# A decoder of two layers on one core: third late projection tile inside attention, POOL's bias adds moved, expert output banks counted free earlier

## The chip, the cores and the metric

One core of one Trainium2 chip runs the kernel. Times are device microseconds (us) of one execution. The kernel is compared by the median of several executions.

## The reference

x has 2 batches of 1024 rows and 256 columns; a context has 2 batches of 77 rows. Six sublayers follow one another, each `x = layernorm(x + sublayer(x))`:

```python
x = _layernorm(x + _L0_attn_ref(...))    # quaternion projections, 16 heads, softmax over 1024 keys
x = _layernorm(x + _L0_xattn_ref(...))   # two hops of memory attention over the context
x = _layernorm(x + _L0_ffn_ref(...))     # 8 experts: gelu(tok @ w1 + b1) @ w2 + b2, 256 rows each
x = _layernorm(x + _L1_attn_ref(...))    # long convolution, gelu, projection, layer norm
x = _layernorm(x + _L1_xattn_ref(...))   # 16 heads, keys and values from the context
x = _layernorm(x + _L1_ffn_ref(...))     # quantised gated feed-forward
```

In the first attention q and k are quaternion-normalised, the scores are scaled by 1/4, a constant is added to them, and the output goes through a quaternion projection with a bias (`ob`). The experts add a first bias inside the gelu and a second one (`b2`) to the output.

## The kernel before, in words

The program is written engine by engine: each engine has one list of instructions, executed in order, and semaphores (`wait_ge`, `then_inc`) tie them. Nothing is planned by a compiler; the order in each list is the schedule. x stays in SBUF as 16 tiles X[:, t] of 128 rows.

**Projections ahead of attention.** For t below HT = 14, PE transposes tile t (`x_turn`, L1472), projects queries and keys together (L1482) and values (L1485); ACT copies the transposed tile (`x_evac`, L550) and the values (`v_evac`, L554); DVE adds the bias to queries and keys (`biased`, L848), releasing `qk_biased`, for which PE's `project(t + 2)` waits. For t below TB = 8 (the first batch) the norm follows in the same loop: squares (ACT), sums (POOL, L399 and L403), root (ACT), reciprocal and product (DVE, `normed`), then the split into a high and a low float16 part. At t = 9 to 11 DVE stages the copies of unit 0 (`stage_queries` L879, `stage_keys` L887, `stage_values` L906, which gives semaphore `vs`). POOL goes on to `late_norm(8)` and `late_norm(9)` (L415 to L420: square, two sums) as soon as their biased tiles are there. After its loop ACT computes one small Exp (L603), which loads the Exp table, and then the first exponential.

**Attention units.** The attention runs in UN = 16 units of two heads, units 0 to 7 on batch 0 and 8 to 15 on batch 1. A unit has 8 key tiles kt. For each kt PE computes two groups of scores (`scores`, L1498), three groups ahead, in three pairs of banks; ACT takes the exponential of each (L599, 128x1024, 256 in all); PE multiplies with the values (`values`, L1512) into bank 6. At the end of a unit DVE copies bank 6 away (L1038, `o_evac`), for which the next unit's first `values` waits. In between DVE stages the next unit's queries, keys and values; SP transposes the staged queries and keys by DMA (L312, L317); the next unit's scores wait for them. `stage_queries(8)`, in unit 7, waits for the low part of every tile.

**Late tiles.** Tiles HT to 15 are projected within units 0 to 5, one tile per three units, through bank 7: `late_turn` (PE, L1519), `late_x` (DVE copy), six `late_project` pieces (PE, L1530) at the steps of SPREAD, counted in key tiles from the tile's first unit, as (k half, matrix q/k/v), `late_biased` (DVE, L932) before the value pieces, `late_v` (DVE). The second batch's norms are `late_qn` (DVE, L941 to L949), one per unit from unit 0 and the tiles from HT on together in unit HT - 8; POOL makes the sums before (`late_norm`) and the low part behind (`late_low`, L429) each. In units 1 to 9 DVE also quantises the last layer's weights in three parts per matrix.

**Bias of the output.** Behind the last `late_low` POOL adds the output bias to X in four adds of four tiles (L439, `x_plus_bo`). From unit 8 on the heads of batch 0 are normalised (`first_heads`, which gives `att`), turned, projected and added to X (`out_residual`, L1001 to L1010, waits for all four adds); `ln_power` on POOL gives the reciprocal deviations.

**The experts' entry.** After the memory attention PE transposes x by groups (L1672), computes context keys (L1757) and values in five chunks (`context_values`, L1767), and `hidden(0)`, L1790. DVE forms the masked keys (L1144, L1146: eight products per half), then per chunk of values a bias add and masked products (L1154, L1156), giving `l1_kv` once for the keys and once per chunk (6 in all); then the powers of the convolution (L1165 scans, L1169) and `ffn_y_free` by 2. POOL adds the second bias to x in eight adds (L470, `x_plus_b2`) as soon as x is transposed. PE's order is hidden(0), context_values(2) (needs one `l1_kv`), context_values(3), hidden(1), output(0) (L1802; needs `ffn_y_free` >= 1 and `l1_kv` >= 4), output(1), hidden(2), hidden(3), output(2) (needs `ffn_y_free` >= 3) and so on. `expert_stats(e)` on DVE (L1194) adds an output to x after `x_plus_b2`, and gives `ffn_y_free` one more.

The line that sets today's release of the output banks stands behind the scans:

```python
            for k in range(KD):
                ins = dve.tensor_scalar(CBrev[:, k, :], Apow[:, k, ::-1], convC[:, k:k + 1], convB[:, k:k + 1], ALU.mult, ALU.mult)
            link(ins)
            ...
            dve.sem_inc(sem("ffn_y_free"), 2)
```

Of the kernel before, what the change touches and what calls it, by code (L numbers as in the profile page):

```python
# [11 lines left out]
ACT = mybir.ActivationFunctionType  # L12
ALU = mybir.AluOpType
# [3 lines left out]
P = 128  # L17
B, L, D = 2, 1024, 256
T = B * L // P
TB = T // B  # L20
# [14 lines left out]
G4 = T // 4  # L35
# [14 lines left out]
LN_CN = tuple(range(LN_C, LN_C + E - 2)) + (LN_C + E, LN_C + E + 3)  # L50
LN_DN = (LN_CN[6] - 2, LN_CN[6] - 1, LN_CN[7] - 2, LN_CN[7] - 1) + tuple(range(LN_CN[7] + 1, LN_E))

HT = 14
SPREAD = {3: (0, 0), 6: (1, 0), 9: (0, 1), 12: (1, 1), 16: (0, 2), 19: (1, 2)}

UX = T * KD
AHEAD = 3
# [21 lines left out]
def decoder(nc, a, out):  # L79
    w_kept = nc.dram_tensor("w_kept", (P, 18, D), F32, kind="Internal").ap()  # L80
    with ExitStack() as ctx:
        sems = {}

        def sem(name):
            if name not in sems:
                sems[name] = ctx.enter_context(nc.semaphore(name))
            return sems[name]
# [25 lines left out]
        X = keep(T, D)  # L113
# [245 lines left out]
        def _(pool):  # L359
# [14 lines left out]
            def ln_power(step, n, at=0):  # L374

                pool.wait_ge(sem("ln_stat"), step + 1)
                pool.tensor_scalar(veps[:, at:at + n], mv[:, at:at + n, 1], LN_EPS, None, ALU.add).then_inc(sem("ln_eps"), 1)  # L377
                pool.wait_ge(sem("ln_eps"), step + 1)
                pool.tensor_tensor(rstd[:, at:at + n], veps[:, at:at + n], expo[:, at:at + n], ALU.pow).then_inc(sem("ln_rstd"), 1)  # L379
# [29 lines left out]
            def late_norm(t):  # L409

                pool.wait_ge(sem("qk_biased"), t + 1)
                pool.wait_ge(sem("nrm"), min(t - 1, TB))
                pool.wait_ge(sem("qn"), t - 1)
                qk = qk_sb[t].rearrange("p m c d -> p (m c d)")
                pool.tensor_tensor(sq[t % 2], qk, qk, ALU.mult).then_inc(sem("sq"), 1)  # L415
                pool.wait_ge(sem("sq"), t + 1)
                s4 = sq[t % 2].rearrange("p (m c d) -> p m c d", m=2, c=NQ)
                pool.tensor_tensor(s4[:, :, 0:2], s4[:, :, 0:2], s4[:, :, 2:4], ALU.add).then_inc(sem("n2_half"), 1)
                pool.wait_ge(sem("n2_half"), t + 1)
                pool.tensor_tensor(n2[t % 2], s4[:, :, 0], s4[:, :, 1], ALU.add).then_inc(sem("n2"), 1)  # L420

            def late_low(t):
# [6 lines left out]
                    ins = pool.tensor_tensor(lo, src[:, m], hi, ALU.subtract)  # L429
                ins.then_inc(sem("qk_lo"), 1)  # L430

            late_norm(TB)
            for t in range(TB, T):
                if t + 1 < T:
                    late_norm(t + 1)
                late_low(t)
            pool.wait_ge(sem("x_tr"), T)
            for g in range(G4):
                ins = pool.tensor_tensor(X[:, 4 * g:4 * g + 4, :], X[:, 4 * g:4 * g + 4, :],  # L439
                                         bq4[:, 3:4, :].to_broadcast([P, 4, D]), ALU.add)  # L440
                ins.then_inc(sem("x_plus_bo"), 1)
            for q in range(8):
                ln_power(LN_A + q, 2, 2 * (q % 2))
            for hop in range(2):
                for g in range(G4):
# [19 lines left out]
                                   pattern=[[-P, i1 - i0], [LC, HC]], channel_multiplier=-1).then_inc(sem("l1_mask"), 1)  # L465

            pool.wait_ge(sem("ffn_b_in"), 16)
            for e in range(E):
                pool.wait_ge(sem("xg_tr"), FFN_X + e // 2 + 1)
                pool.tensor_tensor(X[:, 2 * e:2 * e + 2, :], X[:, 2 * e:2 * e + 2, :],  # L470
                                   b2b[:, e:e + 1, :].to_broadcast([P, 2, D]), ALU.add).then_inc(sem("x_plus_b2"), 1)
# [59 lines left out]
        def _(act):  # L531
# [46 lines left out]
            for t in range(HT):  # L578
                if t + 1 < HT:
                    x_evac(t + 1)  # L580
                if t == TB:
                    norm(TB - 1)
                if 3 <= t < TB:
                    high(t - 3)
                if t < TB:
                    square(t)
                v_evac(t)
                if 1 <= t < TB:
                    norm(t - 1)
                if t in (TB - 1, TB):  # L590
                    high(t - 2)

            def exps(u, kt):
                for half in range(2):
# [4 lines left out]
                    act.activation(PT[kt % 2][:, half], PS[:, 2 * (n % 3):2 * (n % 3) + 2, :], ACT.Exp,  # L599
                                   scale=DH ** -0.5 / QK_UP ** 2).then_inc(sem("exp_done"), 1)  # L600

            act.activation(jred, jred, ACT.Exp)  # L603
            for u in range(UN):
                for kt in range(TB):
                    exps(u, kt)
# [197 lines left out]
        def _(dve):  # L804
# [190 lines left out]
            def out_residual(r, b):  # L995

                t = TB * (r // 4) + r % 4
                dve.wait_ge(sem("wo_mm"), r + 1)
                dve.wait_ge(sem("x_plus_bo"), G4)
                xv = X[:, t:t + 5:4, :]  # L1000
                link(dve.tensor_tensor(xv, bank(b).rearrange("p (h d) -> p h d", h=2), xv, ALU.add))  # L1001
                stats((pair(r), 2), 2 * (r % 2)).then_inc(sem("ln_stat"), 1)
# [5 lines left out]
            def attn_unit(u):  # L1008
                if u + 1 < UN:
                    stage_queries(u + 1)  # L1010
                    stage_keys(u + 1)
                    stage_values(u + 1)
                if 1 <= u <= 9:
                    quantised((u - 1) // 3, (u - 1) % 3)
                late = HT + u // 3
                if late < T and u % 3 == 0:
                    late_x(late)
                if u < HT - TB:
                    late_qn(TB + u)
                if u == HT - TB:  # L1020
                    for t in range(HT, T):
                        late_qn(t)
                if late < T and u % 3 == 1:
                    late_biased(late)
                if late < T and u % 3 == 2:
                    late_v(late)
                if u >= NP:
                    q = (u - NP) // 2
                    if u % 2 == 0:
                        if q >= 1:  # L1030
                            out_norm(q - 1)
                        first_heads(q, 0)
                        first_heads(q, 1)
                    else:
                        first_turned(q)
                        out_residual(q, 7)
                dve.wait_ge(sem("pv_done"), TB * u + TB)
                dve.tensor_copy(OSB[:, u], bank(6)).then_inc(sem("o_evac"), 1)  # L1038
# [99 lines left out]

            dve.wait_ge(sem("l1_mask"), 8)
            for c in range(KD):
                dve.wait_ge(sem("l1_k_mm"), 1)
# [29 lines left out]
            def convolved(n, part):  # L1173
# [10 lines left out]
                else:  # L1184
                    link(dve.tensor_tensor(z, r, CBrev[:, k, :], ALU.mult))
                    dve.scalar_tensor_tensor(r, xt, convD[:, k:k + 1], z, ALU.mult, ALU.add).then_inc(sem("conv"), 1)

            dve.sem_inc(sem("ffn_y_free"), 2)  # L1188

            def expert_stats(e, at=0):  # L1190
                dve.wait_ge(sem("ffn_y_mm"), e + 2)
# [271 lines left out]
        def _(pe):  # L1463
# [103 lines left out]
            def attn_unit(u):  # L1567
                for kt in range(TB):
                    for n in range(2 * (TB * u + kt) + 3, 2 * (TB * u + kt) + 5):
                        if n < 2 * TB * UN:  # L1570
                            scores(n)
                    late, step = HT + u // 3, TB * (u % 3) + kt
                    if late < T and step == 0:
                        late_turn(late)
                    values(u, kt)
                    if late < T and step in SPREAD:
                        late_project(late, *SPREAD[step])
                    if u >= NP:
                        first_out((u - NP) // 2, TB * (u % 2) + kt)
# [473 lines left out]
```

## Time and profile before

| what | us |
|---|---|
| median of 3 runs (839.37 to 842.55) | 841.64 |
| the profiled execution | 846.17 |
| its span, first to last instruction | 844.2 |
| PE busy | 733.6 (87%) |
| ACT busy | 542.9 (64%) |
| DVE busy | 544.0 (64%) |
| POOL busy | 199.0 (24%) |
| mean granted TensorE clock | 0.949 |

The profile is one execution. A timeline row gives the start, the length, the engine, the line and operation, what is written and read, the number of instructions merged into the row, and in brackets the idle time before it with what ended it. Line 12 of the kernel is L12.
### The profile page before, as it was taken

How to read it: one execution, taken by the hardware profiler on the slowest of the kernel's cores; microseconds unless marked ns; L12 is line 12 of the kernel's file. 1: busy time of each engine (PE TensorE's matmuls, PEld its weight loads, DVE VectorE, ACT ScalarE, POOL GpSimd, SP SyncE). 2: the span in 40 equal slices, each digit the busy share in tenths (PEclk: the TensorE clock that was granted, in tenths of full speed). 3: DMA queues.
4: the chain of work that ended last, by engine and by line, in shares of the span. 5: the costliest groups of instructions: out<-in, count | busy, mean ns of one | idle time of the engine just before them, and what ended most of it. 6: DMA issues, size and time to landing. Idle time of an engine off the chain costs nothing.

```text
span 844.2 us, 10886 instructions
## 1 busy us (share of the span) xinstructions
PE 733.6 (87%) x3860; PEld 405.0 (48%) x3860; DVE 544.0 (64%) x1203; ACT 542.9 (64%) x912; POOL 199.0 (24%) x237
## 2 busy tenths in 40 slices
PE   3998999989999989999799998678798999993497
PEld 2652222212222228887688886344444754441386
DVE  4683747674232227879414739859977487888886
ACT  3639999989999973414132152565787453698991
POOL 1661131250000003025004013375554200000012
PEclk9899999999999999999899999589999899997598
DMA  7311214123272422020145000002100000000002
GB/s 203 104 25 31 46 26 89 26 63 51 63 224 51 96 74 70 32 91 10 32 168 200 0 1 1 0 0 76 35 5 0 2 1 0 1 0 0 1 25 75
DMA packets 57373, 42.13 MB, mean 50 GB/s; under 512 B 36866, under 2 KB 54120, under 8 KB 57192
## 3 DMA queue, kind: packets, MB, share of 16 engines
q1 hardware_dynamic: 57176, 41.31, 17.5%
q8 instruction: 31, 0.51, 0.3%
q14 instruction: 22, 0.18, 0.1%
q10 hardware_dynamic: 144, 0.13, 0.1%
HBM read 28.59 MB, written 4.46 MB: 39 GB/s over the span
## 4 chain that ended last, share of the span: by engine, by line
PE 53%; ACT 21%; DVE 18%; issue 4%; POOL 2%; DMA 1%; SPq 1%; POOLq 0%; DVEq 0%; ACTq 0%
ACT arena L599 14%; PE banks L2017 7%; PE banks L1512 6%; PE banks L2025 5%; PE banks L1802 5%; PE banks L1790 5%; PE banks L1498 3%; PE banks L1482 3%; DVE arena L961 2%; DVE arena L969 2%; DVE arena L1342 2%; PE banks L1699 2%; PE banks L1917 2%; PE banks L1860 1%; ACT arena L777 1%
## 5 line engine op out<-in xcount | busy, mean ns | idle before, releaser
L599 ACT ACTIVATE arena<-banks 128x1024 f32<-128x1024 f32 x256 | 239.3, 1049 | 7.6 <-PE banks L1512 6.4
L1512 PE MATMUL banks<-arena 128*32 128x512 f32 x1024 | 136.4, 604 | 2.3 <-DVE arena L1038 2.1
L1498 PE MATMUL banks<-arena 64*128 64x512 f16 x512 | 87.8, 384 | 15.1 <-ACT arena L599 7.9
L377 POOL TENSOR_SCALAR arena<-arena 128x2 f32<-128x2 f32 (+1 forms) x38 | 11.9, 314 | 347.7 <-DVE arena L964 347.7
L2017 PE MATMUL banks<-arena 128*128 128x512 f32 x192 | 83.1, 594 | 1.1 <-DVE arena L1358 0.9
L1498 PEld LDWEIGHTS banks<-arena 64*128 64x128 f16 x512 | 21.3, 93 | 118.9 <-ACT arena L599 105.5
L690 ACT ACTIVATE arena<-banks,arena 128x77 f32<-128x77 f32 x256 | 59.1, 365 | 23.2 <-DVE arena L1266 23.2
L2025 PE MATMUL banks<-arena 128*128 128x256 f32 x192 | 44.4, 396 | 26.8 <-ACT arena L798 26.8
L1802 PE MATMUL banks<-arena 128*128 128x256 f32 x256 | 57.8, 387 | 5.8 <-DVEq L1188 5.8
L2017 PEld LDWEIGHTS banks<-arena 128*128 128x128 f32 x192 | 36.2, 190 | 47.4 <-issue 43.4
L499 POOL TENSOR_TENSOR arena<-arena 128x616 f32<-128x616 f32 x32 | 42.2, 1320 | 60.0 <-DVE arena L1274 59.9
L1790 PE MATMUL banks<-arena 128*128 128x256 f32 x256 | 56.2, 379 | 0.0
L1802 PEld LDWEIGHTS banks<-arena 128*128 128x128 f32 x256 | 49.6, 195 | 13.1 <-issue 6.2
L969 DVE TENSOR_SCALAR arena<-arena 128x256 f32<-128x256 f32 x96 | 45.6, 528 | 13.7 <-POOL arena L379 13.5
L2025 PEld LDWEIGHTS banks<-arena 128*128 128x128 f32 x192 | 38.3, 200 | 33.3 <-ACT arena L798 27.6
L660 ACT ACTIVATE arena<-banks,arena 128x256 f32<-128x256 f32 x64 | 26.2, 474 | 40.3 <-PE banks L1790 40.2
L1790 PEld LDWEIGHTS banks<-arena 128*128 128x128 f32 x256 | 48.6, 190 | 6.6
L756 ACT ACTIVATE arena<-banks 128x512 f32<-128x512 f32 x48 | 28.2, 612 | 30.4 <-PE banks L2017 30.4
L616 ACT ACTIVATE arena<-banks 128x1024 f32<-128x1024 f32 x18 | 18.5, 1029 | 44.7 <-PE banks L1672 38.9
L1038 DVE COPY arena<-banks 128x512 f32<-128x512 f32 x16 | 10.9, 683 | 51.0 <-PE banks L1512 51.0
L1875 PE MATMUL banks<-arena 64*128 64x308 f32 x128 | 30.1, 552 | 15.7 <-ACT arena L690 12.6
L961 DVE BATCH_NORM_STATS2 arena<-arena 128x6 f32<-128x256 f32 x112 | 40.2, 414 | 1.2
(252 smaller groups left out, 1313.6 us busy)
## 6 DMA issues: line engine op xcount, KB each, us to landing
arena<-in_L_ffn_w SPq DMA_DIRECT2D x16, 1024.0 KB, 7.5
w_kept<-arena SPq DMA_DIRECT2D x3, 768.0 KB, 3.6
arena<-w_kept SPq DMA_DIRECT2D x3, 768.0 KB, 5.0
arena<-in_x SPq DMA_DIRECT2D x4, 512.0 KB, 8.6
out_x<-arena SPq DMA_DIRECT2D x3, 512.0 KB, 2.9
arena<-in_L_ffn_b SPq DMA_DIRECT2D x1, 1024.0 KB, 9.0
arena<-in_L_ffn_w_gate SPq DMA_DIRECT2D x1, 768.0 KB, 8.3
arena<-in_L_ffn_w_up SPq DMA_DIRECT2D x1, 768.0 KB, 10.0
```

The lines of the kernel that those rows point to most:

```text
L499: pool.tensor_tensor(Ex[n % 4], Ex[n % 4], rdx[:, n % 4, :, None].to_broadcast([P, HC, LC]), ALU.mult).then_inc(sem("xa_w"), 1)
L599: act.activation(PT[kt % 2][:, half], PS[:, 2 * (n % 3):2 * (n % 3) + 2, :], ACT.Exp, scale=DH ** -0.5 / QK_UP ** 2).then_inc(sem("exp_don ...
L690: ins = act.activation(Ex[n % 4][:, h, :], PS[:, 2 * (n % 2) + h // 4, LC * (h % 4):LC * (h % 4) + LC], ACT.Exp, scale=-1.0, bias=mxs[:, 8 ...
L961: ins = dve.bn_stats(bstat[:, at + j, :], view(j))
L969: ins = dve.tensor_scalar(dst(j), src(j), mv[:, at + j, 0:1], rstd[:, at + j:at + j + 1], ALU.subtract, ALU.mult)
L1498: mm = pe.matmul(bank(2 * (n % 3) + h), KT[u % 2][64 * h:64 * h + 64, P * kt:P * kt + P], QT[u % 2][64 * h:64 * h + 64, 512 * half:512 * h ...
L1512: mm = pe.matmul(PS[32 * j:32 * j + 32, 6, :], VS[w][:, kt, h, :], PT[kt % 2][:, half, h, :], start=(kt == 0), stop=(kt == TB - 1))
L1790: mm = pe.matmul(PS[:, f // 2, 256 * (f % 2):256 * (f % 2) + 256], W1r[r][:, k, P * f:P * f + P], XT[:, k, TE * P * e:TE * P * e + TE * P] ...
L1802: mm = pe.matmul(bank(4 + e % 2)[:, D * j:D * j + D], hT[e % 2][:, f, P * j:P * j + P], W2r[r][:, f, :], start=(f == 0), stop=(f == FT - 1))
L1875: mm = pe.matmul(PS[:, 2 * (n % 2) + q, 0:4 * LC], qTx[g % 2][rows, k, P * j:P * j + P], Kbd[rows, k, g // 2, 4 * q:4 * q + 4, :].rearrang ...
L2017: mm = pe.matmul(bank(2 + n % 4), (wgT if n < IC * G4 else wuT)[:, k, P * c:P * c + P], XT[:, k, 512 * g:512 * g + 512], start=(k == 0), s ...
L2025: mm = pe.matmul(PS[:, t % 8 // 2, D * (t % 2):D * (t % 2) + D], UF[:, c, P * t:P * t + P], wdT[:, c, :], start=(c == 0), stop=(c == IC - 1))
```

## The change

- HT is 13: tile 13 is projected within attention too. A late tile now takes two units (tile 13 units 0 and 1, tile 14 units 2 and 3, tile 15 units 4 and 5), with its six pieces at steps 2, 4, 6, 8, 11 and 13 of 16. DVE's late norms of tiles 13 and 14 come in unit 5, that of tile 15 in unit 6.
- POOL waits for `vs` before its first `late_norm`.
- The four adds of the output bias move: two behind the low parts of tiles 10 and 12, two behind `att` 2 and 4, before the first two `ln_power`. `out_residual` waits for two of them for the pairs of tiles 0 to 7, for four behind.
- ACT's small Exp moves into the projection loop, at t = 9.
- POOL waits for `l1_kv` 6 before the eight adds of the second bias.
- DVE counts both output banks free ahead of the masked keys.

```diff
-HT = 14
-SPREAD = {3: (0, 0), 6: (1, 0), 9: (0, 1), 12: (1, 1), 16: (0, 2), 19: (1, 2)}
+HT = 13
+SPREAD = {2: (0, 0), 4: (1, 0), 6: (0, 1), 8: (1, 1), 11: (0, 2), 13: (1, 2)}
@@ gpsimd
+            def x_plus_bias(g):
+                pool.wait_ge(sem("x_tr"), 4 * g + 4)
+                pool.tensor_tensor(X[:, 4 * g:4 * g + 4, :], X[:, 4 * g:4 * g + 4, :],
+                                   bq4[:, 3:4, :].to_broadcast([P, 4, D]), ALU.add).then_inc(sem("x_plus_bo"), 1)
+
+            pool.wait_ge(sem("vs"), 1)
             late_norm(TB)
             for t in range(TB, T):
                 if t + 1 < T:
                     late_norm(t + 1)
                 late_low(t)
-            pool.wait_ge(sem("x_tr"), T)
-            for g in range(G4):
-                ins = pool.tensor_tensor(X[:, 4 * g:4 * g + 4, :], X[:, 4 * g:4 * g + 4, :],
-                                         bq4[:, 3:4, :].to_broadcast([P, 4, D]), ALU.add)
-                ins.then_inc(sem("x_plus_bo"), 1)
+                if t in (TB + 2, TB + 4):
+                    x_plus_bias((t - TB) // 2 - 1)
             for q in range(8):
+                if q < 2:
+                    pool.wait_ge(sem("att"), 2 * q + 2)
+                    x_plus_bias(2 + q)
                 ln_power(LN_A + q, 2, 2 * (q % 2))
...
             pool.wait_ge(sem("ffn_b_in"), 16)
+            pool.wait_ge(sem("l1_kv"), 6)
             for e in range(E):
@@ scalar
                 if t in (TB - 1, TB):
                     high(t - 2)
+                if t == TB + 1:
+                    act.wait_ge(sem("j_exp"), 1)
+                    act.activation(jred, jred, ACT.Exp)
...
-            act.activation(jred, jred, ACT.Exp)
             for u in range(UN):
@@ vector
-                dve.wait_ge(sem("x_plus_bo"), G4)
+                dve.wait_ge(sem("x_plus_bo"), G4 if r >= 4 else 2)
...
-                late = HT + u // 3
-                if late < T and u % 3 == 0:
+                late = HT + u // 2
+                if late < T and u % 2 == 0:
                     late_x(late)
+                if late < T and u % 2 == 1:
+                    late_biased(late)
                 if u < HT - TB:
                     late_qn(TB + u)
-                if u == HT - TB:
-                    for t in range(HT, T):
+                if u in (HT - TB, HT - TB + 1):
+                    for t in range(HT, T - 1) if u == HT - TB else (T - 1,):
                         late_qn(t)
-                if late < T and u % 3 == 1:
-                    late_biased(late)
-                if late < T and u % 3 == 2:
+                if late < T and u % 2 == 1:
                     late_v(late)
...
+            dve.sem_inc(sem("ffn_y_free"), 2)
             dve.wait_ge(sem("l1_mask"), 8)
...
-            dve.sem_inc(sem("ffn_y_free"), 2)
@@ tensor
-                    late, step = HT + u // 3, TB * (u % 3) + kt
+                    late, step = HT + u // 2, TB * (u % 2) + kt
```

## Rows read from the trace of the kernel before

**Rows 1.** Timeline of PE, 50 to 66 us: start, us, engine, line, op [idle before].
```profile
57.17 1.96 PE L1482 MATMUL banks<-arena 128*128 128x512 f32 x4 [1.01 <-ACT arena L550]
...
59.83 1.88 PE L1482 MATMUL banks<-arena 128*128 128x512 f32 x4
...
63.09 0.82 PE L1498 MATMUL banks<-arena 64*128 64x512 f16 x6 [0.52 <-issue]
```

**Rows 2.** Timeline of ACT around its first attention exponential.
```profile
62.61 0.39 ACT L554 ACTIVATE arena<-banks 128x256 f32<-128x256 f32 x1 [2.20 <-PE banks L1485]
63.01 1.28 ACT L603 ACT_TABLE_LOAD   x1
...
64.42 11.30 ACT L599 ACTIVATE arena<-banks 128x1024 f32<-128x1024 f32 x12
```

**Rows 3.** Timeline of DVE, 54 to 58 us.
```profile
54.31 2.16 DVE L879 COPY arena<-arena 128x256 f16<-128x256 f16 x4
56.40 0.68 DVE L848 TENSOR_TENSOR arena<-banks,arena 128x512 f32<-128x512 f32 x1
57.00 0.61 DVE L887 COPY arena<-arena 128x256 f16<-128x256 f16 x4
```

**Rows 4.** Timeline of DVE: ends of units 2, 5 and 6, first copy of unit 7.
```profile
111.46 0.69 DVE L1038 COPY arena<-banks 128x512 f32<-128x512 f32 x1 [5.71 <-PE banks L1512]
...
156.91 0.69 DVE L1038 COPY arena<-banks 128x512 f32<-128x512 f32 x1 [5.71 <-PE banks L1512]
...
171.58 0.69 DVE L1038 COPY arena<-banks 128x512 f32<-128x512 f32 x1 [0.84 <-PE banks L1512]
172.19 9.32 DVE L879 COPY arena<-arena 128x256 f16<-128x256 f16 x4
```

**Rows 5.** Timeline of POOL in unit 7.
```profile
172.08 9.34 POOL L439 TENSOR_TENSOR arena<-arena 128x1024 f32<-128x1024 f32 x4
```

**Rows 6.** Timeline of ACT at the change from unit 7 to unit 8.
```profile
187.57 13.14 ACT L599 ACTIVATE arena<-banks 128x1024 f32<-128x1024 f32 x14 [2.83 <-PE banks L1512]
```

**Rows 7.** Timeline of PE at the experts' entry.
```profile
393.12 4.05 PE L1767 MATMUL banks<-arena 128*104 128x256 f32 x16 [1.15 <-DVEq L1148]
...
409.92 15.71 PE L1802 MATMUL banks<-arena 128*128 128x256 f32 x64 [5.84 <-DVEq L1188]
```

**Rows 8.** Timeline of DVE at the experts' entry.
```profile
381.24 9.46 DVE L1146 TENSOR_SCALAR arena<-arena 128x154 f32<-128x154 f32 x8
...
391.15 1.77 DVE L1146 TENSOR_SCALAR arena<-arena 128x154 f32<-128x154 f32 x8
...
403.54 4.50 DVE L1165 TENSOR_TENSOR_SCAN arena<-arena 128x1023 f32<-128x1023 f32 x2
```

**Rows 9.** Timeline of POOL at the experts' entry.
```profile
380.76 9.85 POOL L470 TENSOR_TENSOR arena<-arena 128x512 f32<-128x512 f32 x8
```

**Rows 10.** PE in stretches: us, busy (x instructions), granted clock, DMA share, GB/s.
```profile
400.00:406.50 6.50, 4.08 (x19) 1.00 0.00 0
406.50:413.30 6.80, 3.38 (x8) 0.50 0.01 2
```

**Rows 11.** Critical chain: an attention transpose from issue to landing.
```profile
182.86 3.10 DMA arena<-arena
```

**Rows 12.** Timeline of PE in unit 3: values (L1512) and one late projection (L1530).
```profile
112.53 1.06 PE L1512 MATMUL banks<-arena 128*32 128x512 f32 x8
...
114.06 1.07 PE L1512 MATMUL banks<-arena 128*32 128x512 f32 x8
...
118.87 0.70 PE L1530 MATMUL banks<-arena 128*128 128x256 f32 x2
```

**Rows 13.** Timeline of DVE in unit 6: starts of two late norms, last cast.
```profile
160.79 0.22 DVE L941 TENSOR_SCALAR arena<-arena 128x128 f32<-128x128 f32 x1
...
165.32 0.22 DVE L941 TENSOR_SCALAR arena<-arena 128x128 f32<-128x128 f32 x1
...
170.31 0.43 DVE L949 CAST arena<-arena 128x512 f16<-128x512 f32 x1
```

## The prediction

> **What bounds the kernel now.** I read the timelines engine by engine at the places the diff touches, and beside them what ended each idle time. A measurement of this kernel can tell about 0.5% (4.2 us) from no change. The attention stretch (64 to 313 us) is set by ACT's 256 exponentials; PE runs just below it. Where PE has a backlog, values follow values after 1.53 us (112.53 to 114.06, [rows 12]), while a clean unit lasts 14.67 us (156.91 to 171.58, [rows 4]), or 1.83 per key tile: PE has 0.30 to spare in each, 2.4 per unit. The experts' stage is PE alone. So a microsecond counts if it delays the first exponential, makes ACT idle, or makes PE idle at the experts' entry. Four places do.
>
> **1. The front of attention.** PE's projection of tile 12 waits 1.01 us [rows 1]. The view names ACT's copy, but that was long done; the bias add of tile 10 on DVE, 56.40 to 57.08 [rows 3], is what project(12) also waits for. It is late because four staging copies took 2.16 us, where four of the same size a little later took 0.61 [rows 3]: in the code POOL's squares and sums of tile 8 and 9 run just then. The change holds POOL back until `vs`, so DVE is 1.5 us earlier and tile 12 follows tile 11 at once, 1.01 earlier, and a further 0.4 (an estimate) because the transposes of tile 13 no longer stand between them: 1.4 gained, start at about 55.8. One tile less stands ahead: 59.83 minus 57.17 = 2.66 [rows 1]. Then ACT's value copy ends at 63.00, the Exp table takes 1.28 and the first exponential starts at 64.42 [rows 2], while its scores began at 63.09 [rows 1] and could have been used some 0.45 later, at 63.54. The table moves to tile 9's place, where ACT idles between copies: 0.88 gained. Sum 4.9, first exponential at about 59.5. What is next: the transposed keys. DVE stages them by about 55.5, and an attention transpose lands 3.10 after its issue [rows 11], so 58.6, half a microsecond before the value copy of tile 12 (about 59.0). Bounds: 3.5 if they come a microsecond or more late, 4.9.
>
> **2. A third tile inside attention.** Two tiles were woven into units 0 to 5. Units 3 to 5 took 156.91 minus 111.46 = 45.45 [rows 4]; three clean ones take 44.01: a tile costs 1.44. The third tile is as much PE work again: six pieces of up to 0.70 [rows 12] and a transpose, some 4.2, of which at least 1.44 is exposed. The pieces now stand two key tiles apart, and 2 x 0.30 gives back just one piece, so each is met with nothing saved up, and one still falls on key tile 6 and one on 0, beside the hand-over of bank 6. I take 1.9 per tile, nearer to the row than to the 4.2: 3 x 1.9 - 2 x 1.44 = +2.8. Bounds +1.4 (all as cheap as now) and +9.7 (3 x 4.2 - 2.88, nothing hidden). With part 1 the shorter front is worth only 2.1.
>
> **3. The stall before unit 8.** In unit 7 the four query copies take 9.32 us [rows 4] instead of 0.61, beside POOL's four adds of the output bias to x, 9.34 [rows 5]. Keys and queries of unit 8 are transposed late and ACT idles 2.83 [rows 6]. The adds go: two of 2.3 us behind POOL's low parts in units 2 and 4, when DVE mostly waits for PE, two behind `att` in units 8 and 10, when DVE has only the unit's last copy left. `out_residual` now asks for two before tile 8, enough for rows of tiles 0 to 7. Gain 2.8; below it 2.0, if the adds brush the next staging copies, which have about 12 us until they are needed.
>
> **4. Unit 5 on DVE.** Late norms of tiles 13 and 14 move there from unit 6, where two norms filled DVE from 156.91 to 170.74 [rows 4, 13], 13.8 us. Unit 5 adds the bias add (0.68, [rows 3]) and, an estimate of that size, 0.9 for the value copy and a longer quantising part: 15.4. POOL now also computes tile 15's norm beside it. One low part on POOL stretched a norm from 4.53 (160.79 to 165.32) to 5.42 (165.32 to 170.74) [rows 13]; a norm has three POOL instructions where the low part has two, so I add 1.4: 16.8 against a unit of 15.6. The copy of bank 6 comes 1.2 late, PE's values of unit 6 queue behind it with the later scores, and the exponentials wait: +1.2. Bounds 0 (no contention) and +2.5 (twice my stretch). By the Trainium skill (SBUF — State Buffer, "Who interferes with whom") the shared port pair is an exclusive lock, and a DVE instruction with two SBUF inputs blocks until a GpSimd instruction that reads SBUF is over; by that rule the three instructions could hold DVE for all their length, some 2.2, and the sum would be 0.8 worse. The row only shows that the slowing exists, not that all of it is lost.
>
> **5. The experts' entry.** POOL's eight adds, 9.85 [rows 9], run beside DVE's mask products: eight take 9.46, the next eight, alone, 1.77 [rows 8]. The change puts the adds behind the last `l1_kv`, so DVE is 7.7 earlier and PE's 1.15 before context_values(2) goes [rows 7]. output(0) waited 5.84 [rows 7] for `ffn_y_free`, which DVE gave after its two scans (4.50, [rows 8]); now it is given ahead of everything and only the fourth `l1_kv` is left, some 10 us earlier than PE asks. PE starts output(0) at 409.92 - 5.84 - 1.15 = 402.9. Clock: the granted clock was 0.50 (1.2 GHz) from 406.5 to 413.3 after 1.00 before it, with PE busy only 3.38 of those 6.8 us [rows 10]; idle 404.1 to 409.9 is the only large gap nearby. Output(0) ran 3.4 us at half pace, losing 1.7. Gain 5.84 + 1.15 + 1.7 = 8.7, lower bound 7.0. The adds now cost beside DVE's scans: all eight over by about 408, DVE too, even if each scan waits for an add; the first sum is asked for when output(0) ends, at about 409.8, and nothing on PE waits for that sum until output(2), 27 us later. So it costs nothing.
>
> **Sum.** -4.9 + 2.8 - 2.8 + 1.2 - 8.7 = -12.4. The profiled execution took 846.17 us in all (span 844.2); it becomes 833.8. It was 4.5 above the median of the three timed runs, 841.64, so for the median I expect 829.2. Clock stretches behind the entry may fall differently as all moves earlier: one of 6.8 us at half speed costs up to 3.4; I allow 2 either way.
>
> **Rivals.**
> - *The third tile is dear*: PE never catches up in units 0 to 5, and the tile costs 7 instead of 2.8. For it: 2 x 0.30 against 0.63 to 0.70 a piece, and the turn at key tile 0. Against: 14.4 us spare in six units for 12.6 of work. -12.4 + 4.2 = -8.2: 833.4. Chance 0.13.
> - *The entry gives back part*: DVE's scans and scalings, crossed with POOL's adds, end so late that the chain of sums slips, or the half clock comes elsewhere: entry worth 4. -7.7: 833.9. Against: 27 us of room. Chance 0.08.
> - *The change does not do what it says*: the adds only move the stall, because the first two run into the next unit's staging. Then -2.8 is missing: 832.0. Chance 0.05.
> - *Slower*: PE stands at late_project's first piece (key tile 2 of units 0, 2, 4), in order, waiting for DVE's copy of x, and with it all scores. DVE reaches that copy behind staging and the quantiser, about 4.8 after the unit's first copy; PE asks at about 5.6. If staging beside POOL is slow each time, every further microsecond stops ACT. It turns the sum only from 4.1 us per unit on (12.4 / 3); for more than 0.5%, 5.5. Three such holds of 6 give -12.4 + 18 = +5.6: 847.2. Against: staging needs only 0.6 per four copies and POOL is idle at those starts, save in unit 0. Chance 0.02.
>
> **How the numbers follow.** Forecast 829.2 with 0.72, its own bounds about 825 to 833. The range 825.0 to 834.5 takes in most of the two 833s. Faster by over 0.5% (under 837.4): 0.94; within: 0.04; slower: 0.02.
>
> **What would show it.** First exponential at about 59.5 and no table load before it; PE's idle before tile 12 gone; units 0 to 4 about 15.3 to 15.7 long; DVE's copies in unit 7 at 0.61 and ACT not idle there; the copy of bank 6 after unit 5 about 1 us late; output(0) starting with no idle time and no half clock behind it, both sets of mask products at 1.8. The forecast is wrong if units 0 to 5 grow by more than 5 us together, or if PE idles elsewhere between 400 and 470 us.

## The result and the profile after

The changed kernel takes 828.2 us (median; 827.9 to 830.37) against 841.39 for the kernel before (839.37 to 842.55): ratio 0.9835, interval 0.9804 to 0.9865. Timed once more on another chip it took 827.15 against 843.71, ratio 0.9802 (0.977 to 0.9833). The forecast was 829.2.

The profiled execution took 828.11 us, the one before 846.17; that is 18.1 between single executions where the medians differ by 13.2 and 16.6, and part of the excess is clock, as shown below. The page after: span, busy time of each engine.

```profile
span 826.4 us, 10898 instructions
...
PE 729.3 (88%) x3864; PEld 402.0 (49%) x3864; DVE 532.4 (64%) x1205; ACT 542.5 (66%) x910; POOL 202.6 (25%) x237
```

I cut both traces at the same events. "First" and "last" are the starts of ACT's first and last attention exponential; hidden(0) and hidden(2) the starts of those expert matmuls on PE; gates the first matmul of the last feed-forward.

| stretch, us | before | after | saved |
|---|---|---|---|
| start to tile 3's projection | 27.26 | 24.28 | 3.0 |
| tile 3 to first exponential | 37.2 | 32.1 | 5.1 |
| units 0 to 5 | 90.85 | 91.91 | -1.1 |
| unit 6 | 14.63 | 17.13 | -2.5 |
| unit 7 | 17.67 | 14.67 | 3.0 |
| units 8 to 15 (to the last exponential) | 122.7 | 122.9 | -0.2 |
| last exponential to hidden(0) | 74.61 | 73.45 | 1.2 |
| hidden(0) to hidden(2) | 40.56 | 31.08 | 9.5 |
| hidden(2) to gates | 258.0 | 258.1 | -0.1 |
| gates to end | 160.8 | 160.8 | 0.0 |

The first line is not the change: nothing that runs there was touched. Before, tile 2 was projected at the half clock (3.78 us for its four matmuls, 1.98 after) and tile 3 started 3 us later; after, the half clock lay on tile 0, and tile 2 still had to wait 1.55 us for ACT's copy. The line to hidden(0) is of that kind too: before, a half clock lay at 355.3 to 358.7 us, and none after; the kernels of runs 6 and 7 below, whose code in this stretch is the old one, took 73.44 and 73.45. Without these two the change is worth about 13.7 in this pair.

**The front.** PE after, columns as in [rows 1]:

```profile
50.07 1.88 PE L1489 MATMUL banks<-arena 128*128 128x512 f32 x4
...
52.65 1.88 PE L1489 MATMUL banks<-arena 128*128 128x512 f32 x4
...
55.91 0.82 PE L1505 MATMUL banks<-arena 64*128 64x512 f16 x6 [0.52 <-ACT arena L561]
```

and ACT after, which answers to [rows 2]:

```profile
47.53 1.28 ACT L601 ACT_TABLE_LOAD   x1
...
55.43 0.39 ACT L561 ACTIVATE arena<-banks 128x256 f32<-128x256 f32 x1 [2.20 <-PE banks L1492]
56.34 14.26 ACT L609 ACTIVATE arena<-banks 128x1024 f32<-128x1024 f32 x15 [0.53 <-PE banks L1505]
```

From tile 11's projection to tile 12's are 2.58 us, where there were 3.97 (53.20 to 57.17); the scores come 0.1 behind the value copy, and the table was loaded at 47.53, between copies. Value copy's end to first exponential is 0.5 instead of 1.4. DVE shows where POOL's norms of tiles 8 and 9 went:

```profile
49.89 0.64 DVE L887 COPY arena<-arena 128x256 f16<-128x256 f16 x4
...
55.17 2.25 DVE L887 COPY arena<-arena 128x256 f16<-128x256 f16 x4
57.34 1.42 DVE L895 COPY arena<-arena 128x256 f16<-128x256 f16 x4
```

The first four staging copies are at 0.64 instead of 2.16 [rows 3], and now the eight of unit 1 take 2.25 and 1.42. They are needed 12 us later, so nobody waits.

**Unit 5 and 6.** DVE after: the first row of the norm of tile 14, two rows of it under contention, its cast, and the copy of bank 6.

```profile
144.30 0.22 DVE L949 TENSOR_SCALAR arena<-arena 128x128 f32<-128x128 f32 x1
...
145.95 1.01 DVE L953 TENSOR_TENSOR arena<-arena 128x128 f32<-128x128 f32 x1
147.00 0.77 DVE L954 SCALAR_TENSOR_TENSOR arena<-arena 128x128 f32<-128x128 f32 x1
...
150.70 0.43 DVE L957 CAST arena<-arena 128x512 f16<-128x512 f32 x1
...
151.38 0.68 DVE L1046 COPY arena<-banks 128x512 f32<-128x512 f32 x1
```

POOL beside it: low part of tile 13, then square and sums of tile 15.

```profile
144.47 1.30 POOL L429 TENSOR_TENSOR arena<-arena 128x256 f16<-128x256 f32 x2 [10.05 <-DVE arena L957]
145.72 1.09 POOL L415 TENSOR_TENSOR arena<-arena 128x512 f32<-128x512 f32 x1
...
147.70 0.46 POOL L420 TENSOR_TENSOR arena<-arena 128x128 f32<-128x128 f32 x1
```

PE behind it, and its clock in stretches:

```profile
152.21 1.12 PE L1519 MATMUL banks<-arena 128*32 128x512 f32 x8 [1.57 <-DVE arena L1046]
...
154.22 1.94 PE L1519 MATMUL banks<-arena 128*32 128x512 f32 x8
```
```profile
148.00:152.80 4.80, 3.07 (x28) 1.00 0.00 0
152.90:156.30 3.40, 3.40 (x18) 0.53 0.62 120
```

The norm takes 6.7 us (144.30 to 151.04), where the longer one before took 5.42 [rows 13]; the copy of bank 6 comes at 151.38, and PE waits 1.57 for it. ACT's fifth exponential of unit 6 is 1.54 late (the expectation of run 1 calls it the fourth). Then a stretch at 0.53 follows, in which values take 1.94 instead of 1.06, and another 1.1 is lost.

**Unit 7.** The first four copies:

```profile
167.67 0.62 DVE L887 COPY arena<-arena 128x256 f16<-128x256 f16 x4
```

0.62 against 9.32 [rows 4], and the unit takes 14.67 us.

**The experts' entry.** PE after, then DVE and POOL, which answer to [rows 7], [rows 8] and [rows 9]:

```profile
383.30 3.62 PE L1774 MATMUL banks<-arena 128*104 128x256 f32 x16
386.75 7.07 PE L1797 MATMUL banks<-arena 128*128 128x256 f32 x32
393.66 13.98 PE L1809 MATMUL banks<-arena 128*128 128x256 f32 x64
407.47 13.98 PE L1797 MATMUL banks<-arena 128*128 128x256 f32 x64
```
```profile
372.73 1.77 DVE L1155 TENSOR_SCALAR arena<-arena 128x154 f32<-128x154 f32 x8
...
374.94 1.77 DVE L1155 TENSOR_SCALAR arena<-arena 128x154 f32<-128x154 f32 x8
...
389.43 5.50 DVE L1174 TENSOR_TENSOR_SCAN arena<-arena 128x1023 f32<-128x1023 f32 x2
...
394.97 3.25 DVE L1178 TENSOR_SCALAR arena<-arena 128x1024 f32<-128x1024 f32 x2
400.83 0.69 DVE L1201 TENSOR_TENSOR arena<-banks,arena 128x512 f32<-128x512 f32 x1 [2.61 <-issue]
```
```profile
389.45 14.80 POOL L477 TENSOR_TENSOR arena<-arena 128x512 f32<-128x512 f32 x8 [17.17 <-issue]
```

PE goes from chunk to hidden(1) to output(0) with no bracket of idle time, and output(0) and output(1) take 13.98 instead of 15.71: no half clock. Both sets of mask products take 1.77. The eight adds have moved beside the scans and cost there: scans 5.50 for 4.50, the scalings behind them 3.25 for 1.53, and the adds themselves 14.80 instead of 9.85. The first sum on DVE still starts at 400.83, when output(0) is just done.

### The profile page after: what moved, and what is told of

Same layout as the page of the kernel before. It is cut to its first block, busy times and chain, and to the rows that moved or that the text cites. A ratio compares the mean times of both kernels' runs of the same rounds, so it can differ in the third digit from the quotient of the medians.

```text
span 826.4 us, 10898 instructions
## 1 busy us (share of the span) xinstructions
PE 729.3 (88%) x3864; PEld 402.0 (49%) x3864; DVE 532.4 (64%) x1205; ACT 542.5 (66%) x910; POOL 202.6 (25%) x237
## 4 chain that ended last, share of the span: by engine, by line
PE 58%; ACT 18%; DVE 17%; issue 3%; POOL 2%; SPq 1%; DMA 1%; POOLq 0%; DVEq 0%; ACTq 0%
ACT arena L609 12%; PE banks L1519 8%; PE banks L2024 7%; PE banks L1797 7%; PE banks L2032 5%; PE banks L1809 5%; PE banks L1505 3%; PE banks L1489 2%; DVE arena L969 2%; DVE arena L977 2%; DVE arena L1349 2%; PE banks L1706 2%; PE banks L1924 2%; PE banks L1867 1%; PE banks L1679 1%
## 5 line engine op out<-in xcount | busy, mean ns | idle before, releaser
L377 POOL TENSOR_SCALAR arena<-arena 128x2 f32<-128x2 f32 (+1 forms) x38 | 10.7, 281 | 280.1 <-DVE arena L972 280.1
L2032 PE MATMUL banks<-arena 128*128 128x256 f32 x192 | 44.4, 396 | 26.8 <-ACT arena L806 26.8
L1797 PE MATMUL banks<-arena 128*128 128x256 f32 x256 | 56.2, 379 | 0.0
L1809 PE MATMUL banks<-arena 128*128 128x256 f32 x256 | 56.1, 379 | 0.0
L1519 PEld LDWEIGHTS banks<-arena 128*32 128x32 f32 x1024 | 20.5, 108 | 45.1 <-issue 43.2
```

The source lines that it names most:

```text
L1519: mm = pe.matmul(PS[32 * j:32 * j + 32, 6, :], VS[w][:, kt, h, :], PT[kt % 2][:, half, h, :], start=(kt == 0), stop=(kt == TB - 1))
L1797: mm = pe.matmul(PS[:, f // 2, 256 * (f % 2):256 * (f % 2) + 256], W1r[r][:, k, P * f:P * f + P], XT[:, k, TE * P * e:TE * P * e + TE * P] ...
L1809: mm = pe.matmul(bank(4 + e % 2)[:, D * j:D * j + D], hT[e % 2][:, f, P * j:P * j + P], W2r[r][:, f, :], start=(f == 0), stop=(f == FT - 1))
L2032: mm = pe.matmul(PS[:, t % 8 // 2, D * (t % 2):D * (t % 2) + D], UF[:, c, P * t:P * t + P], wdT[:, c, :], start=(c == 0), stop=(c == IC - 1))
```

## The experiments

All kernels are compared with the kernel before on the same chip. "The changed kernel" is the one after. In each of the three groups of runs (1, 3, 4, 5; then 2, 6, 7, 8; then 9) the kernel before took 843.7 us.

**1. Late norm of tile 14 in unit 6.**

```diff
-                    for t in range(HT, T - 1) if u == HT - TB else (T - 1,):
+                    for t in (HT,) if u == HT - TB else range(HT + 1, T):
```

> The changed kernel, but DVE's late norm of tile 14 is computed in unit 6 beside that of tile 15, not in unit 5. Theory (unit 5 overfills DVE): the copy of bank 6 after unit 5 comes on time, ACT no longer loses 1.54 us at the fourth exponential of unit 6, and the half clock of 153 to 156 us, with its 1.02, goes too: unit 6 takes 14.7 to 15.1 instead of 17.1 us, and the kernel is 2 to 2.5 us faster than the changed one, 826. Rival (POOL's sums set it, DVE only follows): the same 1.5 us appear one unit later, at the start of unit 7, and nothing is gained.

Measured: 822.44 us, ratio 0.9731 (0.9696 to 0.9766). Unit 6 takes 14.60, unit 7 14.66, and no wait appears in either. The rival is out: what was late was DVE in unit 5. The ratio is further from the changed kernel's than the 2.5 us of unit 6; in the profiles 3.6 of the rest lie between hidden(2) and the gates (254.5 instead of 258.1), where the code is the same; run 9 comes back to this. A half clock fell into unit 0 here (16.4 instead of 15.06), as in the profiles of runs 3, 6 and 7 (16.2 to 16.3). Before the change unit 0 took 14.99 and in run 6, with the same code up to there, 16.23: where such stretches fall differs from one execution to the next.

**2. POOL's sums later, DVE's work unchanged.** This separates the two reasons that DVE could be late in unit 5.

```diff
-                if t + 1 < T:
+                if t + 1 < T and t != T - 2:
                     late_norm(t + 1)
                 late_low(t)
+                if t == T - 2:
+                    late_norm(t + 1)
```

> The changed kernel, but POOL does tile 15's squares and sums behind the low part of tile 14, not before it, so that nothing but one low part runs beside DVE's norm of tile 14 in unit 5. The DVE work in unit 5 is the same. Theory A (contention makes the copy of bank 6 late): the norm of tile 14 takes 5.4 instead of 6.7 us, PE waits 0.2 to 0.5 instead of 1.57 and unit 6 is 14.8 to 15.0 with no half clock. Theory B (DVE's volume alone makes it late): the norm is as long as before and unit 6 stays at 16.1.

Measured: 823.68 us, ratio 0.977 (0.9736 to 0.9804). DVE, with the cast and the copy of bank 6, and PE:

```profile
145.20 0.67 DVE L954 SCALAR_TENSOR_TENSOR arena<-arena 128x128 f32<-128x128 f32 x1
...
149.24 0.43 DVE L959 CAST arena<-arena 128x512 f16<-128x512 f32 x1
...
149.92 0.68 DVE L1048 COPY arena<-banks 128x512 f32<-128x512 f32 x1
```
```profile
150.75 1.06 PE L1521 MATMUL banks<-arena 128*32 128x512 f32 x8 [0.18 <-DVE arena L1048]
```

The norm takes 5.35 (144.24 to 149.59), PE waits 0.18, unit 6 is 14.68. Theory A: unit 5's DVE work fits, just; POOL's three instructions beside it made it late.

**3. HT 14 with all other edits.**

```diff
-HT = 13
-SPREAD = {2: (0, 0), 4: (1, 0), 6: (0, 1), 8: (1, 1), 11: (0, 2), 13: (1, 2)}
+HT = 14
+SPREAD = {3: (0, 0), 6: (1, 0), 9: (0, 1), 12: (1, 1), 16: (0, 2), 19: (1, 2)}
...
-                late = HT + u // 2
+                late = HT + u // 3
```

> The changed kernel with HT 14, the old steps of SPREAD and three units per late tile; all other edits stay. Theory (by the two traces the third tile saves 2.7 in front, costs 1.0 in units 0 to 5 and 2.5 in unit 6): no gain from the third tile, this is 0.8 faster than the changed kernel to 0.5 slower, with the first exponential 2.7 later and unit 6 at 14.7. Rival (the third tile is what brings the attention's gain): 3 us slower than the changed kernel.

Measured: 829.7 us, ratio 0.9827 (0.9801 to 0.9853), no different from the changed kernel's; unit 6 is 14.63, unit 7 14.67. The latter shows that the stall before unit 8 goes without HT 13; of the edits left, the moved adds are the one that touches unit 7. The comparison with the changed kernel is in run 9.

**4. Both entry edits undone.**

```diff
-            pool.wait_ge(sem("l1_kv"), 6)
...
-            dve.sem_inc(sem("ffn_y_free"), 2)
             dve.wait_ge(sem("l1_mask"), 8)
...
+            dve.sem_inc(sem("ffn_y_free"), 2)
             def expert_stats(e, at=0):
```

> The changed kernel with both edits of the experts' entry undone: the output banks are counted free behind the scans again, and POOL's eight adds wait for nothing. Theory: PE idles 5.8 us before output(0) and 1.15 before the third chunk of context values, and a half clock may follow: 7.0 to 8.9 us slower than the changed kernel, 835 to 837. Rival (the DVE work merely moves, the experts start earlier but wait later): under 4 us slower.

Measured: 837.6 us, ratio 0.9936 (0.9912 to 0.996). PE in that kernel, then a stretch with the busy time of PE, its weight loads, DVE, ACT and POOL before the clock:

```profile
384.58 4.05 PE L1774 MATMUL banks<-arena 128*104 128x256 f32 x16 [1.17 <-DVEq L1155]
...
401.38 16.94 PE L1809 MATMUL banks<-arena 128*128 128x256 f32 x64 [5.84 <-DVEq L1195]
```
```profile
400.40:407.10 6.70, 5.72 (x14) 4.59 (x15) 0.67 (x1) 0.00 (x0) 0.00 (x0) 0.50 0.02 4
```

Hidden(0) to hidden(2) takes 41.81 instead of 31.08: 10.7, above my bound of 8.9. The waits are the same 1.17 and 5.84; 5.7 of the 6.7 us at the half clock here lay on output(0) and output(1), which took 16.94, 3.0 more than 13.98, where in the profile before only 3.4 us of it fell on work. The entry carries most of the change.

**5. The adds in a lump again.**

```diff
-                if t in (TB + 2, TB + 4):
-                    x_plus_bias((t - TB) // 2 - 1)
+            for g in range(G4):
+                x_plus_bias(g)
             for q in range(8):
-                if q < 2:
-                    pool.wait_ge(sem("att"), 2 * q + 2)
-                    x_plus_bias(2 + q)
```

> The changed kernel with the four adds of the output bias in a row behind the last low part, as before the change. Here the last low part comes in the middle of unit 6 (about 160 us), not at its end. Theory (the stall was the adds beside the staging copies of unit 7): the adds run from about 161.6 to 171, cover the staging copies at 167.7, which then take some 4 us, the transposes land in time all the same, since unit 7 ends at 180: no change, within 0.5 us. Rival (the adds cost wherever they stand in a lump): 2.8 us slower, ACT idle before unit 8.

Measured: 826.08 us, ratio 0.9798 (0.9755 to 0.9841), no different from the changed kernel. POOL and DVE:

```profile
161.13 9.35 POOL L434 TENSOR_TENSOR arena<-arena 128x1024 f32<-128x1024 f32 x4
```
```profile
166.15 4.70 DVE L884 COPY arena<-arena 128x256 f16<-128x256 f16 x4
```

The staging takes 4.70 us and unit 7 still 14.67. So the stall had two sufficient cures in this change: the adds elsewhere (run 3), or the last low part 10 us earlier, as the split of the late norms brings it.

**6. Only the release of the banks, on the kernel before.**

```diff
+            dve.sem_inc(sem("ffn_y_free"), 2)
             dve.wait_ge(sem("l1_mask"), 8)
...
-            dve.sem_inc(sem("ffn_y_free"), 2)
```

> The kernel before the change with one edit: DVE counts the output banks free ahead of the masked keys. POOL's adds still run beside the mask products. Theory (the two entry edits overlap: either takes output(0) off the scans): PE still waits 1.15 before the third chunk, output(0) starts behind hidden(1) with no wait, no half clock: 7.5 us faster than before in the experts' entry, masks' first products still 9.5. Rival (the fourth l1_kv becomes the wait in its place): output(0) starts some 2 us or more behind the end of hidden(1).

Measured: 836.49 us, ratio 0.9878 (0.9825 to 0.9931).

```profile
393.98 4.06 PE L1767 MATMUL banks<-arena 128*104 128x256 f32 x16 [1.17 <-DVEq L1149]
...
404.78 13.98 PE L1802 MATMUL banks<-arena 128*128 128x256 f32 x64
```

No idle time before output(0), 1.17 before the third chunk, hidden(0) to hidden(2) 32.85: 7.7 of the 9.5. Its units 7 and 8 are of interest too. The stall is there as in [rows 6], and this time a half clock follows it:

```profile
185.10:191.80 6.70, 6.13 (x26) 0.50 0.27 106
```

Units 7 and 8 take 18.71 and 16.28, 5.1 us more than 14.67 and 15.20 after.

**7. Only POOL's wait, on the kernel before.**

```diff
             pool.wait_ge(sem("ffn_b_in"), 16)
+            pool.wait_ge(sem("l1_kv"), 6)
```

> The kernel before the change with one edit: POOL waits for the last l1_kv before its eight adds. Theory: DVE is 7.7 earlier at the scans, which now run beside the adds and take 5.5 and 3.3 instead of 4.5 and 1.5, so the banks come free at about the time hidden(1) ends plus 2: PE idles 1 to 3 us before output(0) instead of 5.8, none before the third chunk, 4 to 6 us faster than before. Rival (adds beside scans cost as much as beside masks): PE idle as before, 1 us faster.

Measured: 840.9 us, ratio 0.9967 (0.9949 to 0.9984). PE and DVE:

```profile
405.85 16.87 PE L1803 MATMUL banks<-arena 128*128 128x256 f32 x64 [4.70 <-DVEq L1189]
```
```profile
396.76 5.50 DVE L1166 TENSOR_TENSOR_SCAN arena<-arena 128x1023 f32<-128x1023 f32 x2
...
402.29 3.24 DVE L1170 TENSOR_SCALAR arena<-arena 128x1024 f32<-128x1024 f32 x2
```

My size was wrong: I had 4 to 6 us. Counted from hidden(0), the scans start 5.6 us earlier than before (not 7.7, because DVE now waits for PE's third chunk), but they and the scalings take 2.7 longer beside the adds, and PE asks 1.8 earlier. So it still idles 4.70, and output(0) and output(1) take 16.87 with a half clock in them: hidden(0) to hidden(2) 38.84, a gain of 1.7. The two entry edits belong together: the early release makes the later scans harmless, the wait of the adds takes the last 1.15 and what follows it.

**8. Both front edits undone.**

```diff
-            pool.wait_ge(sem("vs"), 1)
...
-                if t == TB + 1:
-                    act.wait_ge(sem("j_exp"), 1)
-                    act.activation(jred, jred, ACT.Exp)
...
+            act.activation(jred, jred, ACT.Exp)
             for u in range(UN):
```

> The changed kernel with both front edits undone: POOL starts tile 8's norm without waiting for vs, and the small Exp stands behind the projection loop again. Theory: DVE's first four staging copies take 2.2 us instead of 0.6, PE waits about 1 us before the projection of tile 12, and 1.5 us lie between ACT's last value copy and the first exponential beyond the scores: the first exponential comes 2.0 to 2.4 us later after the same tile's start; the whole is 2 us slower than the changed kernel, 830. Rival (these waits were covered by the transposed keys): under 0.5.

Measured: 831.22 us, ratio 0.9843 (0.9807 to 0.9879), too near the changed kernel's two ratios to tell 2 us; the profile can:

```profile
51.86 1.88 PE L1486 MATMUL banks<-arena 128*128 128x512 f32 x4
...
55.83 1.95 PE L1486 MATMUL banks<-arena 128*128 128x512 f32 x4 [1.23 <-issue]
...
59.85 0.82 PE L1502 MATMUL banks<-arena 64*128 64x512 f16 x6 [1.20 <-DMA arena<-arena]
```
```profile
59.09 1.28 ACT L608 ACT_TABLE_LOAD   x1
...
60.49 5.79 ACT L605 ACTIVATE arena<-banks 128x1024 f32<-128x1024 f32 x6
```

Tile 11 to tile 12 is 3.97 again, tile 12 to the first exponential 4.66 where it is 3.69 after: 1.39 + 0.97 = 2.4. Here the scores waited for the transposes (59.85, released by a DMA), because the keys were staged late; in the changed kernel they waited for ACT's copy.

**9. The changed kernel, the one of run 2 and the one of run 3, again, on one chip.**

> The changed kernel as it is, beside the next two on one chip. Theory: ratio to the kernel before 0.980 to 0.984; unit 6 at 16.1 us, or 17.1 with a half clock; both edits of the entry give 9.5 to 10.7 between hidden(0) and hidden(2).

> The changed kernel with POOL's norm sums of tile 15 behind the low part of tile 14, once more, beside the changed kernel. Theory: 1.4 us faster than the changed kernel where no half clock falls into unit 6, 2.5 where one does, so a difference of 1.4 to 2.5 in the medians; anything beyond it is the clock's stretches behind 500 us. Rival: the larger distance between the earlier ratios (0.977 against 0.9835, 5.5 us) is real and repeats.

> The changed kernel with HT 14, once more, beside the changed kernel. Theory: the third tile is about neutral as the change places it (2.7 in front against 1.0 in units 0 to 5 and 1.4 to 2.5 in unit 6): within 1 us of the changed kernel, and 1.6 slower than the kernel with POOL's sums later. Rival: the third tile is worth 2 us or more as it stands.

Measured: 827.15 (ratio 0.9802, 0.977 to 0.9833), 822.18 (0.9759, 0.9729 to 0.9789) and 828.19 (0.9819, 0.9792 to 0.9846). Unit 6 takes 17.17, 14.66 and 14.63. Units 0 to 5 take 91.9, 91.9 and 91.1, so the third tile costs 0.8 there and saves 2.8 in front: worth 2.0 once unit 5 is mended, and about nothing as the change places it, where unit 6 costs 1.4, or 2.5 with the half clock. The kernel with POOL's sums later is the fastest I have timed twice; its lead of 5 us in the medians is larger than the 2.5 that attention shows. In the profiles the rest lies far behind: from the last expert matmul to the gates the changed kernel takes 162.0 and this one 158.5, with the same instructions; granted clock there:

```profile
503.00:666.00 163.00, 133.32 (x626) 0.88 0.04 15
```
```profile
501.00:660.00 159.00, 128.63 (x623) 0.91 0.04 16
```

The thirteen profiles fall into two groups here whatever the kernel: from hidden(2) to the gates six took 253.8 to 254.6 us (runs 1, 2, 4, 5, 7 and the second of this group), and seven 257.8 to 258.3, before and after among them. The clocks of the timed executions point the same way: on average 0.9577 for the changed kernel and 0.9624 for this one. Over the 91 timed executions of all kernels, 0.01 less granted clock goes with about 4.9 us more within one kernel, so the clock would account for some 2.3 of the 4.2 us between the two means, an estimate that cannot tell unit 6's half clock from those behind 500 us.

## Why the prediction was right, by its own steps

The total was 1.0 us off the first measured median, 2.1 off the second, and the range held both. Its terms, against the traces:

- **Front, -4.9**: measured 5.1. The three pieces were 1.39 (run 8 gives it back exactly), 2.66 for the tile, 0.9 for the table. With HT 14 and the other edits tile 12 follows tile 11 after 2.80 (run 3), so 1.17 of the 1.39 is POOL's wait and 0.22 the missing transposes; I had 1.01 and 0.4. The transposed keys were not next; the value copy was, as forecast.
- **Third tile, +2.8**: measured +1.1 over units 0 to 5, of which the tile is 0.8 (run 9) and 0.3 comes with the other edits: with HT 14 and all of them these units take 91.11. The step that failed is "each is met with nothing saved up", which made the term too large. A tile in two units costs 1.38 ((91.91 - 6 x 14.63) / 3), less than 1.54 by the same measure in three units. Nor did the dense spacing hurt: units 0, 2 and 4, with the transpose and pieces two key tiles apart, take 15.06, and units 1, 3 and 5 take 15.57. The row of 1.44 was the better guide than the reasoning laid on top of it.
- **Stall, -2.8**: measured 3.0 in unit 7, 2.8 with unit 8, which is 0.2 longer after; and 5.1 for the two where a half clock follows the stall (run 6). That the stall itself brings one was not in my sum.
- **Unit 5, +1.2**: the mechanism was right to the row: bank 6 late, values and exponentials behind it. It cost 1.4 (16.07 against 14.63), and 1.1 more where the half clock followed, which was not in my sum. The stretch I took, 1.4, was measured as 1.3 (6.74 against 5.42). The rule that I quoted from the Trainium skill (SBUF — State Buffer, "Who interferes with whom"), read as DVE held for the whole of POOL's three instructions, was the upper end. DVE's rows of 1.01, 0.77 and 0.50 in place of 0.29 each are 1.4 longer together, less than POOL's 2.3 (1.09, 0.73 and 0.46), and one DVE instruction ends with each of POOL's. Run 2 confirms contention, not volume.
- **Entry, -8.7**: measured 9.5 in this pair, of which 7.8 before output(0) and 1.7 of clock behind it; where the half clock fell on more of the work (run 4), 10.7. Of the 0.8 I missed before output(0), 0.4 is a wait inside the chunks: before, the third and fourth took 4.05 [rows 7] where they now take 3.62, because the fourth waited for DVE as well. The rest is in how idle time is counted, from the end of a matmul as the profile models it: hidden(0) and hidden(1) show 7.07 where the next starts 6.91 behind them, 0.16 for each of the two waits.
- **The adds beside the scans, 0**: right for the end, with a wrong size. I had POOL through at 408, which is 399.5 on the clock of this trace (hidden(0) starts 8.5 earlier); it was through at 404.2, its adds taking 14.80 instead of 9.85. DVE, which I had 7.7 us earlier, reached the scans 5.6 earlier, because it now waits for PE's third chunk. Run 7 shows what both cost where PE does depend on the scans.

With the measured terms the sum is -5.1 + 1.1 - 3.0 + 1.4 - 9.5 + 0.2 (units 8 to 15) = -14.9, and -13.8 with the half clock of unit 6, which both profiles of the changed kernel have; the two comparisons gave 13.2 and 16.6. So I was 1.4 too cautious: 1.7 too dear for the third tile and 0.8 too little for the entry, against 1.3 too little for unit 6. That errors in both directions left the first median 1.0 off is in part luck: the ratio that I forecast, 829.2 to 841.64 or 0.9853, lies inside the first interval and outside the second. The medians' own difference of 3.4 between chips is larger than my error.

Of the rivals, the dear third tile is refuted (1.1, not 7), the entry gave nothing back, and the adds' move did what it says, though it was not the only cure. The wait of late_project for DVE's copy never showed: PE has no idle time before any of its 36 matmuls.

## What to carry to other kernels

When a semaphore says "this buffer is free", give it where that is true, not where the list happens to have room: one count moved ahead of independent work was worth 7.7 us. Two engines that share a port should be scheduled against what is urgent, not against what is idle: the same kind of POOL instructions, one tile's square and sums, cost nothing beside a staging copy that is due 12 us later, and 1.4 us beside a chain that ends with its unit. And before an idle stretch of PE is priced, look at the clock behind it.

## What the runs showed of the hardware

- **A stall of PE can cost more than its length.** A granted clock of 0.50 followed the idle time before output(0) in all three profiles that have it (5.84 us before and in run 4, 4.70 in run 7), that of 3.2 us before unit 8 in two of three (runs 6 and 7, not before), and that of 1.57 us in unit 6 in two of five: unit 6 took 16.07 in the profiles of runs 4, 5 and 8, and 17.13 and 17.17 in both of the changed kernel, with the same wait. The Trainium skill (TensorE: Matmul & The Clock Gate, Part 1) says that the chip's observation is free-running and does not start with the kernel; that the same stall draws a half clock in one execution and not in the next agrees with it.
- **Which engine loses on the shared port depends on what DVE runs.** Beside DVE's mask products POOL's eight adds took 1.26 to 1.27 us each, as long as after the change once DVE's scalings are done, while each product but the first took 1.30 instead of 0.29 to 0.30: POOL lost nothing. Beside the scans the same adds took up to 3.34, and the second scan 3.28 instead of 2.29. The rows give the shortest, the median and the longest in ns: the adds before (L470) and after (L477), and the products beside the adds before (L1146).

```profile
L470 POOL TENSOR_TENSOR arena<-arena x8: 1262/1265/1273, 380.8 to 389.3; 128x512 f32<-128x512 f32 x8
L477 POOL TENSOR_TENSOR arena<-arena x8: 1268/1494/3337, 389.4 to 403.0; 128x512 f32<-128x512 f32 x8
L1146 DVE TENSOR_SCALAR arena<-arena x8: 886/1303/1310, 381.2 to 389.4; 128x154 f32<-128x154 f32 x8
```

By the Trainium skill (SBUF — State Buffer, "Who interferes with whom") the pair of ports is held for the whole instruction; the trace agrees: in both places the two engines end one instruction each in turn.
- **Identical code behind 500 us took 158 or 162 us** in the profiles. Single executions of this kernel can't be compared to better than that without cutting them by stage.
